# A gated-delta layer with its MLP on one core: a new hand-written order of work on all five engines, six steps deep

## What is computed

```python
qkvz = (hidden_states @ w_qkvz.T)            # 32 heads, each q, k, v, z of 64
mixed = conv_general_dilated(concat(q, k, v), conv_w, ...)   # causal, 4 taps, per channel
g = -exp(A_log) * softplus(a + dt_bias);  beta = sigmoid(b)
q = l2norm(q) * DK ** -0.5;  k = l2norm(k)
def step(S, (q_t, k_t, v_t, g_t, b_t)):      # scanned over the 256 tokens
    S = S * exp(g_t)
    delta = (v_t - k_t @ S) * b_t
    S = S + outer(k_t, delta)
    return S, q_t @ S
o = o * rsqrt(mean(o * o) + EPS) * norm_weight * sigmoid(z)
attn = o.reshape(...) @ w_out.T
x = x + layernorm(attn(layernorm(x)));  x = x + layernorm(ffn(layernorm(x)))
```

## Time and profile before

| | |
|---|---|
| three runs, median (lowest to highest) | 3149.84 us (3148.64 to 3151.75) |
| profiled execution, its own time | 3143.98 us |
| its span, first to last instruction | 3142.2 us |
| granted TensorE clock, mean over the span | 0.988 |
| busy over the span: TensorE / its weight loads | 3023.2 us (96%) / 2040.8 us (65%) |
| busy: VectorE / ScalarE / GpSimd | 2390.4 (76%) / 1765.5 (56%) / 1117.6 us (36%) |
| stage 2, from the first projection to the last output projection | 87.8 to 2767.5 us |

### The profile page before, as it was taken

One profiled execution on the slowest core, in us unless ns is written; L12 is line 12 of the kernel. 1 busy time (PEld: TensorE's weight loads), 2 busy tenths in 40 slices (PEclk: granted clock), 3 DMA queues, 4 the chain that ended last, 5 costly groups with the idle time before them and its releaser, 6 DMA issues. The chain is left out here.

```text
span 3142.2 us, 109422 instructions
## 1 busy us (share of the span) xinstructions
PE 3023.2 (96%) x46912; PEld 2040.8 (65%) x46912; DVE 2390.4 (76%) x5674; ACT 1765.5 (56%) x3306; POOL 1117.6 (36%) x904
## 2 busy tenths in 40 slices
PE   6799999999999999999999999999999999789998
PEld 3466666666666666666666666666766666655455
DVE  7578888888788878888878888887888888545644
ACT  5456666665666655666656566665566666333432
POOL 1444444444444444444444444444444444100000
PEclk9899999999999999999999999999999999899999
DMA  5333434344344433433344444333333334300000
GB/s 152 69 62 68 79 65 68 68 86 70 70 70 83 68 68 64 82 63 66 69 85 69 70 70 86 67 67 67 73 69 64 67 69 69 75 14 27 27 21 14
DMA packets 1027793, 208.77 MB, mean 66 GB/s; under 512 B 977904, under 2 KB 998768, under 8 KB 1026160
## 3 DMA queue, kind: packets, MB, share of 16 engines
q1 hardware_dynamic: 1027312, 201.78, 34.9%
HBM read 120.13 MB, written 39.58 MB: 51 GB/s over the span
## 5 line engine op out<-in xcount | busy, mean ns | idle before, releaser
L1317 PE MATMUL bank<-xT,w_sb 128*128 128x512 f32 x2048 | 996.9, 615 | 15.7 <-DVE kq L1082 9.2
L1317 PEld LDWEIGHTS bank<-xT,w_sb 128*128 128x128 f32 x2048 | 359.7, 190 | 355.9 <-issue 311.9
L773 POOL TENSOR_TENSOR kq<-kq,product 128x510 f32<-128x510 f32 (+2 forms) x384 | 437.3, 1146 | 108.9 <-ACT kq L869 94.3
L1082 DVE SCALAR_TENSOR_TENSOR v_c<-bank,cw,v_c 128x510 f32<-128x510 f32 (+2 forms) x384 | 286.3, 746 | 23.0 <-ACT v_c L869 13.1
L1082 DVE SCALAR_TENSOR_TENSOR kq<-bank,cw,kq 128x510 f32<-128x510 f32 (+2 forms) x384 | 283.7, 739 | 23.7 <-ACT kq L869 14.6
L761 POOL TENSOR_TENSOR dec_ap<-gcrow,gcb 128x1024 f32<-128x1024 f32 x64 | 121.8, 1903 | 502.4 <-DMA gcb<-gcb_d 502.4
L1342 PE MATMUL bank<-kq 64*64 64x128 f32 x4096 | 277.9, 270 | 3.4 <-DVE ap_mat L1135 1.9
L1446 PE MATMUL bank<-wo,u_sq 128*128 128x256 f32 x1024 | 261.4, 399 | 11.4 <-DVE u_sq L1168 11.4
L1097 DVE TENSOR_TENSOR prod_un<-a_un,x_un 128x15 f32<-128x15 f32 (+7 forms) x960 | 216.1, 225 | 60.3 <-DMA a_un<-a_d 42.2
L873 ACT ACTIVATE product<-bank,cw 128x512 f32<-128x512 f32 x384 | 257.1, 688 | 2.1 <-PE bank L1317 2.1
L1424 PEld LDWEIGHTS bank<-ap_mat,delta 64*64 64x64 f32 x4096 | 218.3, 135 | 47.0 <-issue 47.0
(11 more groups left out here) (169 smaller groups left out, 5767.3 us busy)
## 6 DMA issues: line engine op xcount, KB each, us to landing
xT<-xT_d SPq DMA_DIRECT2D x64, 512.0 KB, 3.9
gcrow<-gcrow_d SPq DMA_DIRECT2D x128, 256.0 KB, 4.4
v_r<-v_x SPq DMA_DIRECT2D x512, 64.0 KB
a_d<-ap_mat SPq DMA_DIRECT2D x256, 64.0 KB, 3.6
z_t<-z_d SPq DMA_DIRECT2D x256, 64.0 KB, 2.5
w_sb<-in_w_qkvz SPq DMA_DIRECT2D x8, 1024.0 KB, 6.6
x_un<-eye_un SPq DMA_DIRECT2D x64, 128.0 KB, 2.2
a_un<-a_d SPq DMA_DIRECT2D x64, 128.0 KB, 3.5
```

Source lines behind the costliest of these rows:

```text
L773: nc.gpsimd.tensor_tensor(t[:, :, d:SEQ], t[:, :, d:SEQ], prod[:, :, 0:SEQ - d], ALU.add).then_inc(tap_added[i], 1)
L1082: ins = nc.vector.scalar_tensor_tensor(t[:, :, d:SEQ], src[:, :, 0:SEQ - d], cw_two[m.grp % 2][:, w:w + 1], t[:, :, d:SEQ], ALU.mult, ALU.add)
L1317: ins = nc.tensor.matmul(bank[:, :], w_two[m.grp % 2][:, h, s * P:(s + 1) * P], xT[:, h, :], start=(h == 0), stop=(h == HT - 1))
```

## The change

All engines' `turn` functions of stage 2 are written in a new order. With it:

- `DEPTH` is 6. SyncE, VectorE and TensorE now name steps up to s[4] or s[5], GpSimd and ScalarE up to s[2] and s[3]. TensorE has no work for s[0], and its labels are one above VectorE's for the same time. The loop has 69 turns instead of 67.
- `ring` is computed with 2 instead of 18 and the places are new.
- Each substitution column is split into `sub_product` and `sub_rest`, which can be placed separately. The columns now stand behind each other, with a `residual` and an `accumulate` between.
- The semaphores that are signalled change with the waits; ScalarE's `decays` now waits for its `magnitudes`, and TensorE's projection 5 for `accumulate`.

```diff
-        DEPTH = 4
+        DEPTH = 6
...
-            return banks[(18 * m.off + place) % 4]
+            return banks[(2 * m.off + place) % 4]
...
-                        nc.scalar.activation(dec_p[:, :, :], dec_a[:, :, :], ACT.Abs)
+                        nc.scalar.activation(dec_p[:, :, :], dec_a[:, :, :], ACT.Abs).then_inc(mag_done, 1)
...
-                    def substitute(m, part, columns):
...
+                    def sub_product(m, j):
+                        rows, wid, prod = column(m, j)
+                        if j and last_sub[1] == own.turns:
+                            own.need(last_sub[0])
+                        last_prod[:] = own.mark(nc.vector.tensor_tensor(
+                            prod, a_un[:, j + 1:B, j:j + 1].broadcast_to([P, rows, wid]),
+                            x_un[:, j:j + 1, 0:wid].broadcast_to([P, rows, wid]), ALU.mult)), own.turns
+
+                    def sub_rest(m, j):
+                        rows, wid, prod = column(m, j)
+                        if last_prod[1] == own.turns:
+                            own.need(last_prod[0])
+                        rest = x_un[:, j + 1:B, 0:wid]
+                        ins = nc.vector.tensor_tensor(rest, rest, prod, ALU.subtract)
+                        if j in sub_done:
+                            ins.then_inc(sub_done[j], 1)
+                        else:
+                            last_sub[:] = own.mark(ins), own.turns
...
+                            wait_for(pe, acc_done[1], s[2], 1, back=3)
+                            project(s[2], 5, ring(s[2], 3))
```

More of the change, by code:

```diff
@@ L1087, in conv @@
                             ins.then_inc(conv_done[s], 1)
[L1089 to L1105 removed]
+                    last_sub, last_prod = [0, 0], [0, 0]
@@ new lines, in column @@
+                    def column(m, j):
+                        rows, wid = B - 1 - j, j + 1
+                        return rows, wid, prod_un[:, 0:rows * wid].rearrange("u (i j) -> u i j", j=wid)
+                    def sub_product(m, j):
[5 more added lines that the diff above has]
+                            x_un[:, j:j + 1, 0:wid].broadcast_to([P, rows, wid]), ALU.mult)), own.turns
@@ L1451, in turn @@
                     def turn(s):
+                        if s[4]:
+                            wait_for(pe, og_done[0], s[4], 1, back=1)
+                            output(s[4], 0)
+                            wait_for(pe, state_done[0], s[4], 1)
+                            key_state(s[4], 1)
+                        if s[5]:
+                            wait_for(pe, tap_prod[1], s[5], 1, back=-3)
+                            wait_for(pe, og_done[0], s[5], 1)
+                            project_out(s[5], 1, ring(s[5], 1))
@@ new lines, in turn @@
+                        if s[4]:
+                            wait_for(pe, rhs_done[1], s[4], 1)
+                            solve(s[4], 1)
+                        if s[2]:
+                            wait_for(pe, conv_done[1], s[2], 1)
+                            k_tokens(s[2], 0, ring(s[2], 1))
+                        if s[4]:
+                            wait_for(pe, delta_done[1], s[4], 1)
+                            advance(s[4], 1)
+                            output(s[4], 1)
+                            wait_for(pe, state_done[1], s[4], 1)
+                            key_state(s[4], 2)
@@ new lines, in turn @@
+                        if s[4]:
+                            wait_for(pe, delta_done[2], s[4], 1)
+                            advance(s[4], 2)
+                            output(s[4], 2)
+                            wait_for(pe, state_done[2], s[4], 1)
+                            key_state(s[4], 3)
+                        if s[3]:
+                            wait_for(pe, z_in, s[3], 64)
+                            join16_inner(s[3])
+                        if s[2]:
+                            wait_for(pe, tap_added[5], s[2], 1)
+                            wait_for(pe, kt_done[1], s[2], 1)
+                            scores(s[2], 2, ring(s[2], 3))
@@ new lines, in turn @@
+                        if s[4]:
+                            wait_for(pe, rhs_done[3], s[4], 1)
+                            solve(s[4], 3)
+                        if s[3]:
+                            wait_for(pe, p16_done, s[3], 1)
+                            wait_for(pe, x_row_in, s[3], 64)
+                            join16_outer(s[3])
+                        if s[4]:
+                            wait_for(pe, delta_done[3], s[4], 1)
+                            output(s[4], 3)
+                        if s[2]:
+                            wait_for(pe, tap_added[2], s[2], 1)
+                            wait_for(pe, conv_done[4], s[2], 1)
+                            scores(s[2], 0, ring(s[2], 2))
```

671 lines of the change are left out of this document (305 added, 366 removed).

## The result

Slower. Four runs of the changed kernel have their median at 3200.8 us (3197.3 to 3208.2), four of the kernel before on the same chip at 3149.8. The ratio is 1.0164, 95% interval 1.0145 to 1.0183: +51 us, where -90 was forecast. The profiled execution took 3197.3 us, with a span of 3195.5.

The account below looks back on a forecast made before the run. TensorE's own queue was taken as the bound; -1.75 + 0.2 + 0.15 = -1.4 us a turn, -90 over 64 turns, from 3143.98 to 3054, plus 6 for the median: 3060 us, range 3022 to 3125.

Parts of the forecast that it names:

- Grouping on TensorE: TensorE's order: ten full-array groups a turn become four, mode changes fall 20 to 11; -1.75 us a turn, ends 1.5 and 2.0.
- the sign for the lower end: A 32x32 join between 64x64 work taking 1.15 us or more would speak for the lower grouping gain, 1.5 a turn.
- The handoff of the first state: TensorE waits for VectorE's copy of the first updated state: +0.2 us a turn, ends 0 and 0.5.
- The round trip: Substitution units go out and return (z) for the first join; slow transfers delay it: +0.15 us a turn, ends 0 and 1.0.
- the two rivals on it: Unit trip through z sets the turn (0.14, 3122 us), or x's write holds up z's completion (0.11, 3206 us).
- The rival called slower: SyncE's queue: the write of x between z's write and return adds 3.0 us to the trip; 3206 us, chance 0.11.
- Instructions come late: TensorE's run of 240 small products outpaces instruction fetch: holes of 0.5 us, 1.0 a turn; 3124 us, chance 0.04.
- VectorE against GpSimd: Keeping VectorE's adding of squares apart from GpSimd's work returns VectorE a few tenths a turn, which it waits: 0.
- Shared reads block: Adding the squares waits for GpSimd's scaling of q, second sum of squares 0.5 us late; 3092 us, chance 0.04.
- VectorE's queue binds: VectorE's waits in order keep half to all of the 1.4 us gain a turn; 3105 to 3150 us, chance 0.09.
- Six deep: Stage 2's loop grows from 67 to 69 turns, steps not longer in flight; extra of 66.6 us unchanged, within 10: 0.

Follow-up runs that it names:

- state_with_cover: Changed kernel with TensorE's turn end reordered (solve 0, projection 1, update 0, projection 6), ScalarE's delta 0 earlier, VectorE's first-state copy before conv(1): 3156.7 us, ratio 1.0024.

## Why the prediction was wrong

- *Grouping on TensorE*, -1.75 with ends 1.5 and 2.0: right in kind, at the lower end. The sum of the least values fell from 40.49 to 38.96. The nine changes of mode fewer come to 0.17 each, and a 32x32 join between 64x64 work takes 1.13 there, near the 1.15 that the prediction named as the sign for the lower end. The rule of the Trainium skill on changes of tiling mode ("TensorEngine Tiling (Array Packing)", Key Properties) named the right one of the two.
- *The handoff of the first state*, +0.2 with ends 0 and 0.5: mis-sized, 0.9. I had named a late `conv` and not put its duration in. The order showed that `conv(1)` (2.3 us, three operations) stands ahead of the copy in VectorE's list, and that TensorE's update no longer had a projection behind it. `state_with_cover` shows the term: 44 us back, with one more group of full-array work (0.33 a turn) paid out of it.
- *The round trip*, +0.15, and the two rivals on it: the wait for z is 6.1 us in all, 0.1 a turn, and the write of x behind that of z cost nothing that can be seen. But the trip has little room, as the later runs show: with the run broken, TensorE waits for z 0.2 a turn. The rival called slower had put 3206 us on the write of x; that 3200.8 was measured is chance, since the write's wait did not come.
- *Instructions come late*, given 0.04 and 3124 us, and nothing in the sum: this was the main loss, and the step that failed. The working had the right place, the right rows of a piece and 0.5 us a gap. It then let itself be talked out of it: from the 128 KiB of the Trainium skill's page ("Runtime: NRT & Kernel Launch", Instruction fetch mechanics) I concluded that a run of 3.8 pieces is covered. The same page says that the next page is fetched while the current one is executed, which is what the trace shows: one piece ahead, no more. It also says that crossing a border is mostly hidden; here the measurement differs, with gaps at 105 of 323 borders. The trace of the kernel before could have told: its 24 gaps all end 2.2 to 2.8 us after a fetch starts, and its holes at the first join stand late in a run of 320 rows, one of its two longest. The size was also low. I took 0.5 at half of the borders, 1.0 a turn; measured are 1.5 at the borders (83.8 us in the 57.5 turns of that stretch), at most 0.3 by the clock, and 2.0 in all. The wait for z is 0.1 of it, and 0.1 to 0.2 stay unassigned. The prediction's 250 rows a piece leave out the rows that only wait or signal; with them it is 256.
- *VectorE against GpSimd*, 0: right for the time, but the two were not kept apart. Adding the squares takes 683 ns in the median where it took 688, and the median hides two kinds: 56 of the 128 additions take 0.87 to 1.08 us, most of them 1.06, every one beside GpSimd's scaling of q or its clamp, and the 65 with no GpSimd work beside them at most 0.69. Before, none took over 0.9.
- *Shared reads block*, 0.04 and 3092 us: an addition beside GpSimd is 0.4 longer, but the second 32x32 join, ahead of the sums of squares that need it, is longer by 0.05 in the mean and not by 0.5.
- *VectorE's queue binds*, 0.09: not in the changed kernel, where TensorE's waits for it are the first state alone. It decided seven of the experiments.
- *Six deep*, 0: right in kind, with 12 us less of extra, where I had allowed 10.

Together: -1.5 + 0.9 + 2.0, less 0.3 that before had of such losses, gives +1.1 a turn. With the 1.05 of the turn's measured length, 64 times that, less 12, gives +55 us; the profiled executions are 53 apart. So the forecast -1.75 + 0.2 + 0.15 failed by what it left out, 1.8 more of late instructions and the clock, by 0.7 at the first state, and by 0.2 at the grouping. What stays open: whether the gaps could be had back without a group of full-array work in the first part of the loop, and what sets the start of a fetch. No run tried either.

## What to carry to other kernels

Full-array work between small products is also the time in which TensorE's next piece of instructions arrives: before grouping it, count the rows of the longest run of small products that remains, and compare a piece's 256 rows at their pace (3.6 us here) with the time from the start of a fetch to its first use behind a gap (2.2 to 3.4 us) and with how late the fetch starts (here 1.4 us into the piece before, in the median). A cover taken from a handoff has to be replaced, and the producer's list must be read for what stands ahead of the producing instruction. In a schedule that is tight on several engines, follow the turn around a closed loop and ask whether moved work enters it, before counting what it saves elsewhere.

## What the hardware showed that I had not expected

- A piece of TensorE's instructions, though its packet takes 0.9 to 1.5 us in 90 of 100 cases, is used no sooner than 2.2 us after the fetch starts, where it was waited for; the fetch starts 64 to 232 rows ahead of need (5 to 95 in 100 of the pieces of the changed kernel), and only after the border before it.
- The moment is tied to the count of rows from the program's start and not to the work: the same remainder modulo 256 in two programs shifted by 128 rows, if every instruction of the list is counted.
- After a gap of 2.8 us in TensorE's work the granted clock went from 1.00 to 0.50, the 1.2 GHz level, for 6.8 us; after one of 2.2 us it did not. In the kernel before, where no border gap is longer than 1.04 us, it stayed at 1.00 in this stretch.
